# Two graph layers on one core: the factors of the same-graph mask made by GpSimd from per-partition bounds instead of by TensorE from the one-hot rows

## What is computed

```python
h = relu(layernorm(x));  x = x + L0(h, adj)      # gated attention over adj, plus adj @ (h @ W_gcnb)
h = relu(layernorm(x));  x = x + L1(h, adj)

# L1
graph_id = searchsorted(ptr, arange(n), side='right') - 1     # ptr: 33 bounds of 32 graphs
mask = graph_id[:, None] == graph_id[None, :]
a = where(mask, query @ key.T * scale, 0.0)
scores = (a + 2 * adj) * where(mask, 1.0, -1e6)
softmax = softmax(scores, axis=-1) * mask
out = softmax @ value
```

## Time and profile before

| | us |
|---|---|
| median of 3 runs | 233.49 |
| lowest and highest run | 232.44, 234.9 |
| the profiled execution | 232.86 |
| its span in the trace | 231.0 |
| TensorE, matmuls busy | 222.2 |
| VectorE busy | 183.1 |
| ScalarE busy | 160.1 |
| GpSimd busy | 61.9 |

### The profile page before, as it was taken

The page is one execution under the profiler, slowest core; times in us unless marked ns, Lnnn a source line. Parts: engine busy times, 40 slices in busy tenths (PEclk is TensorE's granted clock), DMA queues, the critical chain, the costliest instruction groups (busy, mean ns, idle before and its releaser), DMA issues. The chain is left out here.

```text
span 231.0 us, 5379 instructions
## 1 busy us (share of the span) xinstructions
PE 222.2 (96%) x2042; PEld 194.5 (84%) x2042; DVE 183.1 (79%) x452; ACT 160.1 (69%) x308; POOL 61.9 (27%) x115
## 2 busy tenths in 40 slices
PE   7899999999999999999999999999999999999971
PEld 6788888888888888888888888888888889999951
DVE  2589778899995967599984499987699949997783
ACT  3768835899966764995651794666995855888760
POOL 4525860000034000001910001730012043576540
PEclk9799999999999999999999999999999999999999
DMA  6999399007989100752400000000000000012123
GB/s 186 359 374 386 113 332 387 15 0 248 285 316 386 44 3 0 259 177 111 173 12 4 0 0 4 1 3 0 3 0 0 3 0 4 0 50 79 48 72 128
DMA packets 20092, 26.34 MB, mean 114 GB/s; under 512 B 1889, under 2 KB 11873, under 8 KB 20065
## 3 DMA queue, kind: packets, MB, share of 16 engines
q1 hardware_dynamic: 19376, 25.71, 32.2%
q10 hardware_dynamic: 688, 0.27, 0.4%
HBM read 23.88 MB, written 2.10 MB: 112 GB/s over the span
## 5 line engine op out<-in xcount | busy, mean ns | idle before, releaser
L1091 PE MATMUL bank_a<-hd,e_hi 128*128 128x257 f16 x256 | 70.3, 274 | 0.0
L1089 PE MATMUL bank_a<-hd,e_hi 128*128 128x257 f16 x256 | 69.7, 272 | 0.0
L1093 PE MATMUL bank_a<-hd,e_lo 128*128 128x257 f16 x256 | 69.4, 271 | 0.0
L1065 PE MATMUL bank_b<-hb,adjt 128*128 128x259 f16 (+1 forms) x512 | 66.5, 273 | 0.2 <-DVE xb L1661 0.2
L1065 PEld LDWEIGHTS bank_b<-hb,adjt 128*128 128x128 bf16 x512 | 49.3, 97 | 7.5 <-DVE xb L1661 0.5
L704 ACT ACTIVATE e_hi<-e_slot 128x1024 f16<-128x1024 f32 x32 | 33.6, 1051 | 26.7 <-PE bank_a L1093 15.6
L1669 DVE SCALAR_TENSOR_TENSOR e_slot<-e_slot,adjt 128x1024 f32<-128x1024 f32 x32 | 39.0, 1219 | 9.0 <-ACT e_slot L697 9.0
L1675 DVE SCALAR_TENSOR_TENSOR e_lo<-e_slot,e_hi 128x1024 f16<-128x1024 f32 x32 | 39.0, 1219 | 7.3 <-ACT e_hi L704 7.2
L697 ACT ACTIVATE e_slot<-s_row,nbias 128x512 f32<-128x512 f32 x64 | 42.3, 709 | 0.2
L570 POOL TENSOR_TENSOR rs_all<-veb,half_neg 128x2 f32<-128x2 f32 x8 | 6.6, 823 | 88.2 <-DVE veb L1848 88.2
L1089 PEld LDWEIGHTS bank_a<-hd,e_hi 128*128 128x128 f16 x256 | 24.7, 96 | 4.0
(11 more groups left out here) (238 smaller groups left out, 380.8 us busy)
## 6 DMA issues: line engine op xcount, KB each, us to landing
adjt<-in_adj_t SPq DMA_DIRECT2D x16, 1024.0 KB, 9.1
x_all<-in_x SPq DMA_DIRECT2D x4, 512.0 KB, 5.3
out<-adjt SPq DMA_DIRECT2D x16, 128.0 KB, 1.9
adjt<-in_x SPq DMA_DIRECT2D x3, 512.0 KB, 7.4
diag<-in_adj SPq DMA_DIRECT2D x16, 64.0 KB, 3.6
adjt<-in_x SPq DMA_DIRECT2D x2, 256.0 KB, 3.7
e_slot<-in_L_gnn_W_gcnb ACTq DMA_DIRECT2D x1, 256.0 KB, 4.0
e_slot<-in_W_saT SPq DMA_DIRECT2D x1, 256.0 KB, 4.8
```

The costliest lines, as they stand in the source:

```text
L1065: eng.matmul(B[:, r % 2, 0:cols], adjt_block(k, j, r), hb16[:, j, part, 0:cols], start=(j == 0 and part == 0), stop=(j == NT - 1 and part ...
L1089: eng.matmul(A[:, r, 0:D + 1], high, hd16[:, j, 0, 0:D + 1], start=(j == 0), stop=False, skip_group_check=True)
L1091: eng.matmul(A[:, r, 0:D + 1], high, hd16[:, j, 1, 0:D + 1], start=False, stop=False, skip_group_check=True)
L1093: mm = eng.matmul(A[:, r, 0:D + 1], low, hd16[:, j, 0, 0:D + 1], start=False, stop=(j == NT - 1), skip_group_check=True)
```

## The change

The bounds are loaded a second time, one per partition, in two columns: partition p of column 0 holds ptr[p - 1] (and -1 in partition 0, where a memset leaves it), column 1 holds ptr[p] (and N + 1 in partition 33). A node is in class p if it is at or above column 0 and not at or above column 1. GpSimd converts the bounds to f32, writes the node numbers 0 to 2047 into 34 partitions (into diag, which isn't loaded yet), compares them with both columns, each result times MASK_ROOT, subtracts one from the other (z_same), and adds -MASK_ROOT (z_other). This stands behind `outside(0)` and ahead of the first `inv_new_deviation`. `turn_onehot` with its 16 matmuls and `keep_z` with its 8 activations are gone, ident_b too.

Since diag is used for the node numbers, SP loads the diagonal blocks after the last of GpSimd's instructions (z_made 8); refill(2) now comes ahead of them, refill(3) stays behind them. TensorE's first scores wait for z_made 8 as well. The rest is semaphore counts.

```diff
-        ident_b = sb("ident_b", [P, P], BF16)
+        edges_i = sb("edges_i", [P, 2], I32)
+        edges = sb("edges", [P, 2])
...
 # sync, behind the load of bv_row
+            eng.wait_ge(z_made, 2)
+            eng.dma_start(edges_i[1:CLS, 0:1], ptr.rearrange("(n a) -> n a", a=1)).then_inc(edges_loaded, 16)
+            eng.dma_start(edges_i[0:NP, 1:2], ptr.rearrange("(n a) -> n a", a=1)).then_inc(edges_loaded, 16)
...
+            refill(2)
+
+            eng.wait_ge(z_made, 8)
             for t in range(NT):
                 eng.dma_start(diag[:, t, :], adj[t * P:(t + 1) * P, t * P:(t + 1) * P]).then_inc(diag_loaded, 16)
 
-            refill(2)
             refill(3)
...
 # gpsimd
-            eng.tensor_copy(ident_b[:, :], ident[:, :]).then_inc(col_made, 1)
+            eng.memset(edges_i[:, 0:1], -1).then_inc(z_made, 1)
+            eng.memset(edges_i[:, 1:2], N + 1).then_inc(z_made, 1)
...
             outside(0)
+            node_row = diag[0:CLS, :, :].rearrange("p t n -> p (t n)")
+            eng.wait_ge(edges_loaded, 16 * 2)
+            eng.tensor_copy(edges[:, :], edges_i[:, :]).then_inc(z_made, 1)
+            eng.iota(node_row, pattern=[[1, N]], base=0, channel_multiplier=0,
+                     allow_small_or_imprecise_dtypes=True).then_inc(z_made, 1)
+            eng.wait_ge(z_made, 4)
+            eng.wait_ge(pick_made, 5)
+            eng.tensor_scalar(z_same[0:CLS, :], node_row, edges[0:CLS, 0:1], MASK_ROOT, ALU.is_ge, ALU.mult) \
+               .then_inc(z_made, 1)
+            eng.tensor_scalar(z_other[0:CLS, :], node_row, edges[0:CLS, 1:2], MASK_ROOT, ALU.is_ge, ALU.mult) \
+               .then_inc(z_made, 1)
+            eng.wait_ge(z_made, 6)
+            eng.tensor_tensor(z_same[0:CLS, :], z_same[0:CLS, :], z_other[0:CLS, :], ALU.subtract).then_inc(z_made, 1)
+            eng.wait_ge(z_made, 7)
+            eng.tensor_scalar(z_other[0:CLS, :], z_same[0:CLS, :], -MASK_ROOT, None, ALU.add).then_inc(z_made, 1)
             for k in range(1, NC):
...
 # scalar
-            def keep_z(c):
-                eng.wait_ge(z_summed, c + 1)
-                if c == 0:
-                    eng.wait_ge(pick_made, 5)
-                eng.activation(z_same[0:CLS, c * CW:(c + 1) * CW], L[0:CLS, c % 2, :], ACT.Copy,
-                               scale=MASK_ROOT)
-                eng.activation(z_other[0:CLS, c * CW:(c + 1) * CW], L[0:CLS, c % 2, :], ACT.Copy,
-                               scale=MASK_ROOT, bias=-MASK_ROOT).then_inc(z_kept, 1)
...
-                    if k == 0 and q in (4, 6):
-                        keep_z(q - 4)
-                        keep_z(q - 3)
...
 # tensor
-            def turn_onehot(c):
...
                 if p == 0:
-                    eng.wait_ge(z_kept, NC)
+                    eng.wait_ge(norm_1_made, 3)
...
                     eng.wait_ge(diag_loaded, 16 * NT)
+                    eng.wait_ge(z_made, 8)
...
-                    if q == 3 and place == 0:
-                        eng.wait_ge(norm_1_made, 3)
-                        turn_onehot(0)
-                    if q == 3 and place == 2:
-                        turn_onehot(1)
-                    if q == 5:
-                        turn_onehot(2 + place // 2)
...
-            eng.wait_ge(col_made, 3)
+            eng.wait_ge(col_made, 2)
...
 # vector
-            eng.wait_ge(col_made, 4)
+            eng.wait_ge(col_made, 3)
```

More of the change, by code:

```diff
@@ L335, in two_graph_layers @@
         bias_kept = sem("bias_kept")
-        z_summed = sem("z_summed")
-        z_kept = sem("z_kept")
+        edges_loaded = sem("edges_loaded")
+        z_made = sem("z_made")
         h1_ready = sem("h1_ready")
```

## The result

The changed kernel takes 250.11 us, the median of four runs (247.65 to 252.45), against 234.19 us for the kernel before beside it; the ratio is 1.070, with a 95% interval of 1.065 to 1.076. It is slower by 7%, where 231.8 us was forecast and 239.5 us was the top of the range. The profiled execution took 249.73 us, its span 247.8 us, 16.8 us more than before (231.0).

A forecast was written before the change was run, and what follows sets the result against it. TensorE, busy without gap from 56 to 190 us, was taken as the bound. Its term of -1.72 us, all others 0, took the median 233.49 to 231.8 us; the range was 230.8 to 239.5.

The forecast's parts named there:

- What the new work can hit: GpSimd's four new SBUF readers, from 75.4 us: VectorE taken as not held, 0; SP's delayed loads hidden, 0.
- Rival 1: From 75.4 us GpSimd's readers hold VectorE's mask and low, TensorE stalls before attend(8): priced at 238, chance 0.36.
- way from ga to the end: ga releases keep_a, then attend(8); ga has 1.3 us in hand, so TensorE stalls 12.5 us at most.
- full hold: Rival 1 with VectorE held for each whole reader: den and ga only after 104.4 us, time 242.8.
- milder case: Rival 1 with VectorE held 0.55 of each reader (3.0, 3.0, 2.2, 2.9 us): ga 2 to 3 us late, 234.
- Rival 2: From 75.4 us VectorE has priority, GpSimd's work ends at 114, TensorE stalls 3 us: 234.8, chance 0.12.
- TensorE's term: Main loop, k = 0: 16 one-hot matmuls in four turns go, 0.43 us each, 1.72 us off TensorE.
- rival 3: Last 20 us: the gain doesn't reach the end, a chain being paced by something that doesn't move: 233.5, chance 0.06.
- ScalarE, GpSimd's small edits and the two loads at 0: Eight ScalarE activations removed, GpSimd's copy and memsets changed, SP's two bounds transfers added: all hidden, 0 us.
- SP's order at 0: diag and refill(3) wait for GpSimd's work, refill(3) issued at 104 to 105 us; landing by 119.3, needed at 126.4: 0.

The follow-up runs named there:

- run of iotas: Against the changed kernel: 13 GpSimd iotas of 34x2048, which only write, replace the four readers, mask factors not computed; 235.89 us, ratio 1.011.
- pieces run: Against the changed kernel: each of GpSimd's four readers cut into eight instructions of 256 columns, same place; 237.05 us, ratio 1.012.
- run with the later readers: Against the changed kernel: the four readers stay on GpSimd but stand behind outside(1), with refill(3) ahead of diag; 238.25 us, ratio 1.023.

## Why the prediction was wrong

**The step that failed** is in "What the new work can hit": "I take this row as it stands: VectorE isn't held, 0". It was put at 0 us and is +18.4 us at attend(8), 15.3 in front of the sums and 3.1 behind their start, all of it VectorE's lateness. It rested on one row, L1472 in L557. That row was read as "let through", and could only say "let through from 0.55 on"; and it is of a two-input instruction, while the longest holds fell on one-input ones, for which the prediction had no term. With the readers out, the run gives the forecast's gain back.

**Rival 1** had the right mechanism, place and sign, at a chance of 0.36 and a price of 238, with 242.8 as its upper end. Its way from ga to the end was right: with ga's measured start its own sum gives a stall of 109.99 - 90.59 - 1.3 = 18.1 us and a time of 233.49 - 1.7 + 18.1 = 249.9, against 250.11. What was short is how late ga comes, 104.4 us against 109.99:

- It reckoned with the two-input instructions alone. scales_1, which VectorE runs ahead of mask(9) (from 75.81 us in the kernel before), stands nowhere in its list. The first to be held, and for whole readers, were a cast of four elements and three others of scales_1. That made mask(9) 21.5 us late, where the rival had it begin behind the first reader, at 80.9. The run with the readers behind scales_1 lacks exactly these holds; 6.4 us of the loss go with them. That it comes out at 243.7, near the rival's full hold (242.8), is partly luck: its comparisons held for 4.2 us, where the rival had 5.5.
- Its milder case was too mild: holds of 0.55, 3.0 + 3.0 + 2.2 + 2.9 = 11.1 us, were to make ga only 2 to 3 us late. In the run behind scales_1 holds of 14.7 us left TensorE 10.58 us of wait, so VectorE's room covered about 4 us and not the 8 to 9 of that case.

It looked for the stall in front of attend(8) alone. `keep_b` comes first in VectorE's order, so 15.1 us of it fall in front of the sums; as VectorE works off one list, and ga stands in it behind `keep_b`, that changes the place of the stall and not its total. Nor did the granted clock of 0.50 add to it, as attend(8) had to wait for `keep_a` after the slow sums.

In size the durations matter too. A comparison with a multiply takes 7.17 us, not 5.5, the addition 5.49 (5.3), the subtraction 4.04 (4.0), the iota 1.83 (2.1): the readers sum to 23.9 us against 20.3. L557 does one operation on each element and L635 does two, which may be why; L642, with one, took 5.49 for the same 2048 columns, 0.2 from its forecast.

The Trainium skill, "SBUF — State Buffer" (Who interferes with whom), was named as giving the rival's upper end. The same section lists `copy`, `cast` and `tensor_scalar` too as instructions that can, with suitable operands, take the shared pair; the prediction's account of it left them out, and they were the costliest. The runs agree with its exclusive lock for these (6.90 us for a cast of four elements beside a 7.17 us comparison), and with its exception where GpSimd only writes and VectorE has two SBUF inputs (1.22 us, not held). They differ from "for the whole instruction" where a two-input instruction meets a comparison: 4.2 us of 7.0. The measurement decides, and even so the rule was a better guide than the single row set against it.

**Rival 2** did not come about: the readers themselves weren't stretched (7.17 + 7.16 + 4.04 + 5.49), as VectorE was the one that waited, and they ended at 98.62 us, before rs_all was wanted. Something like it is what the kernel becomes once they are cut in pieces.

**What held:**
- TensorE's term, -1.72. The places without turns stand at 65.22, 67.44, 69.66 and 71.88 us in the changed trace, 2.22 us each, and k = 0 ends 1.8 us earlier. The run without readers (0.990) and the one with them on VectorE (0.993) both show a gain of this size at the end of the kernel, which also closes rival 3.
- ScalarE, GpSimd's small edits and the two loads at 0: all are in the run without readers.
- SP's order at 0: diag at 98.65 and refill(3) at 106.22 us, near the 95.2 and 104 of the forecast, and nobody waited. The run of iotas tests it without the large stall: refill(3) issued at 108.91 us, the sums of k = 2 at 130.63, no wait. In the pieces run, with refill(3) at 126.22 and those sums at 131.46, TensorE waits 2.1 us for adjt.

Not settled: what sets the 0.6 at which a comparison lets two-input instructions through. That the subtraction, which reads twice, holds for almost its whole length, while an iota, which reads nothing, doesn't hold them at all, suggests that it is the part in which the reader fetches; no run tried that by itself, and it is not shown.

## What to carry to other kernels

Before moving work to an idle GpSimd, list every VectorE instruction that will run beside it, the shortest first: a cast of four elements that stands ahead of the critical work cost as much here as the whole GpSimd instruction beside it. GpSimd's idle time was not free, because VectorE had SBUF-to-SBUF work in its order; 4.4 us on a VectorE with some room was better than 23.9 us on a GpSimd with 31.64 us to spare. And one row in which two instructions overlapped bounds a hold on one side only: ask at which point of the longer one the overlap began.

## What the runs showed of the hardware

- VectorE's casts and scalar operations of 128x4 and 128x256 from SBUF to SBUF were held to the very end of a GpSimd reader (6.90 and 7.11 us beside 7.17 and 7.16, 4.00 beside 4.04, 5.22 beside 5.49), and, by iotas that read nothing, up to 1.87 us each. Instructions of one element a partition such as `v_inv` (0.14 us, at 93.49 inside the addition) passed, and so did the reciprocal of 128x4 just ahead of ga in the run with the later readers (0.18 us at 125.44, inside the second comparison, where ga itself took 3.19).
- An instruction that reads one operand from PSUM passed as well: xb at 86.73 us in the run behind scales_1 takes 0.47 us, its usual time, inside the second comparison.
- The hold goes both ways. Cut into pieces, GpSimd's work grew from 23.9 to 42.4 us, some 12 us of it put down to VectorE (a piece of a comparison took 1.13 us at the least and 3.24 at the most); whole, an instruction lost time only at its start (9.21 us against 7.17, behind a running `mask` and `low`).
- GpSimd needed 3.5 ns an element of a partition for a comparison with a multiply (7.17 us for 2048), VectorE 0.6 (1.27 us).
